# A gated sum moved from a stage of its own into the last group of a state-space mixer

## The reference, cut to what matters

```
attn = mixer(x)                     # in-projection, conv, chunked scan, gate, norm, out-projection
f    = ffn(x)                       # Walsh-Hadamard transforms and two small matmuls
h    = x + attn * silu(f)           # "the joining"
out  = layer1(layernorm(h))         # attention and experts, with a gated sum of its own
```

## Time and profile before

| what | value |
|---|---|
| median of 3 runs | 2561.49 us (2558.56 to 2563.39) |
| the profiled execution | 2560.0 us, of which the trace spans 2557.9 us |
| PE busy | 2264.5 us, 89% of the span |
| DVE busy | 1857.7 us, 73% |
| ACT busy | 1427.6 us, 56% |
| POOL busy | 1275.0 us, 50% |
| granted TensorE clock, mean | 0.950 of full speed |

### The profile page before, as it was taken

The page is one execution under the profiler, slowest core; times in us unless marked ns, Lnnn a source line. Parts: engine busy times, 40 slices in busy tenths (PEclk is TensorE's granted clock), DMA queues, the critical chain, the costliest instruction groups (busy, mean ns, idle before and its releaser), DMA issues. The chain is left out here.

```text
span 2557.9 us, 45525 instructions
## 1 busy us (share of the span) xinstructions
PE 2264.5 (89%) x16164; PEld 1796.8 (70%) x16164; DVE 1857.7 (73%) x3274; ACT 1427.6 (56%) x2439; POOL 1275.0 (50%) x1250
## 2 busy tenths in 40 slices
PE   4994899999999999999999972599999996699993
PEld 2784788888888888888888852488888885344432
DVE  5875777777777777777777746677777776777755
ACT  1331787877878787878787741122222224266661
POOL 3453576787767777686876650345545450000000
PEclk9997999999999999999999985799999998799996
DMA  2002112112121121211211111100000002222214
GB/s 89 1 22 109 42 47 81 44 53 81 53 73 53 44 89 47 78 52 44 82 52 53 44 63 38 30 27 28 21 28 28 21 14 78 74 74 76 80 61 136
DMA packets 91519, 141.18 MB, mean 55 GB/s; under 512 B 23328, under 2 KB 60544, under 8 KB 90048
## 3 DMA queue, kind: packets, MB, share of 16 engines
q1 hardware_dynamic: 89280, 133.96, 15.6%
q10 hardware_dynamic: 2048, 4.72, 0.6%
HBM read 118.12 MB, written 20.32 MB: 54 GB/s over the span
## 5 line engine op out<-in xcount | busy, mean ns | idle before, releaser
L1053 DVE SCALAR_TENSOR_TENSOR mix_cv<-mix_pp,mix_cw,mix_cv 128x384 f32<-128x384 f32 (+4 forms) x864 | 490.9, 571 | 219.3 <-ACT mix_cv L981 198.5
L75 PE MATMUL mix_pp<-l0in_XH,mix_w_lo 128*128 128x384 f32 (+2 forms) x576 | 244.3, 424 | 31.1 <-DVE mix_ss L1042 22.9
L1192 POOL TENSOR_TENSOR ffn_hl<-ffn_h,ffn_hh 128x512 fp32r<-128x512 f32 x112 | 144.8, 1293 | 250.1 <-ACT ffn_hh L1250 250.1
L996 ACT ACTIVATE mix_lm<-mix_pd 128x512 f32<-128x512 f32 x256 | 153.3, 599 | 206.0 <-PE mix_pd L895 204.0
L839 POOL TENSOR_TENSOR mix_ce<-mix_ce,mix_cv 128x1024 f32<-128x1024 f32 x112 | 266.8, 2382 | 0.0
L963 PE MATMUL mix_px<-mix_wo,mix_z 128*128 128x256 f32 x1024 | 256.4, 394 | 0.0
L1715 DVE TENSOR_REDUCE att_tops<-att_psc 128x1 f32<-128x512 f32 (+3 forms) x384 | 189.9, 550 | 56.4 <-PE att_psc L1663 32.2
L845 POOL TENSOR_TENSOR mix_zt<-mix_zsq 128x256 f32<-128x256 f32 x128 | 94.2, 736 | 264.0 <-ACT mix_zsq L1004 264.0
L1739 ACT ACTIVATE att_pr<-att_pst 128x1024 f32<-128x1024 f32 (+7 forms) x256 | 156.5, 656 | 104.0 <-PE att_pst L1680 73.6
L1250 ACT ACTIVATE ffn_hh<-ffn_h 128x512 fp32r<-128x512 f32 x112 | 71.1, 635 | 249.0 <-DVE ffn_h L1273 249.0
L981 ACT ACTIVATE mix_cv<-mix_pp,mix_cb,mix_cw 128x384 f32<-128x384 f32 (+1 forms) x288 | 179.0, 622 | 44.8 <-PE mix_pp L77 44.8
(11 more groups left out here) (330 smaller groups left out, 6893.0 us busy)
## 6 DMA issues: line engine op xcount, KB each, us to landing
mix_ce<-ecs SPq DMA_DIRECT2D x112, 512.0 KB, 3.6
mix_w_raw<-in_w_in SPq DMA_DIRECT2D x8, 1280.0 KB, 5.5
a_part<-att_sums SPq DMA_DIRECT2D x32, 256.0 KB, 5.1
ffn_raw<-in_wgu SPq DMA_DIRECT2D x56, 128.0 KB, 2.2
mix_ll<-cs SPq DMA_DIRECT2D x384, 4.0 KB
mix_wo<-in_w_out SPq DMA_DIRECT2D x8, 512.0 KB, 6.4
ffn_draw<-in_wd SPq DMA_DIRECT2D x28, 128.0 KB, 2.1
q<-qkv_part SPq DMA_DIRECT2D x24, 128.0 KB, 1.9
```

The costliest lines, as they stand in the source:

```text
L75: pe.matmul(out, l_lo, r_hi, start=start, stop=False)
L996: act.activation(lm[o][:, 4 * i:4 * i + 4, :].rearrange("p h l -> p (h l)"), pd[:, :], ACT.Exp).then_inc(l_done, 1)
L1053: last = dve.scalar_tensor_tensor(out, of, cw[:, g, ct, 3 - d:4 - d], out, ALU.mult, ALU.add)
```

## The change

The mixer gets the two arrays f (`f_dram`) and x (`x_dram`) in memory, and in its last group (`LAST` = 112) it forms h row by row. For each token tile i = 0 to 15:

- SP loads row i of f and of x into one of two small buffers each (`load_row`). It does so at the head of iteration c = 113 + i, ahead of that iteration's `rl`, `ll` and `ce`; from i = 2 on it first waits for `joined` >= i - 1, which says that row i - 2 no longer needs the buffer. Row 15 is loaded behind the loop.
- ACT applies Silu to f in slot 113 + i, behind the gate's Silu.
- POOL, at the end of slot 114 + i, waits for the row to be final and multiplies it by silu(f), then adds x and raises `joined`.

`combine` and its tensors are gone.

```diff
+        x0, f0 = ([s.sb(f"{n}{j}", [P, D]) for j in range(2)] for n in ("x0", "f0"))
+        LAST = NC - 16
             # sync
+                def load_row(i):
+                    wait(sp, joined, i - 1)
+                    sp.dma_start(f0[i % 2][:, :], f_dram[:, i, :]).then_inc(f_in[i % 2], 16)
+                    sp.dma_start(x0[i % 2][:, :], x_dram[:, i, :]).then_inc(x_in[i % 2], 16)
...
                         load_weights(g + 1)
+                    if c > LAST:
+                        load_row(c - 1 - LAST)
                     at = slice(b * (T // 2) + j * Q, b * (T // 2) + (j + 1) * Q)
                     wait(sp, d_done, 2 * (c - 1))
                     sp.dma_start(rl[c % 2][0:3, :, :], ...
...
+                load_row(15)
             # gpsimd, at the end of a slot
+                    if LAST <= c - 2 < NC:
+                        i = c - 2 - LAST
+                        pool.wait_ge(acc_done, c - 1)
+                        pool.wait_ge(swished, i + 1)
+                        pool.tensor_tensor(ACC[:, i, :], ACC[:, i, :], f0[i % 2][:, :], ALU.mult).then_inc(product, 1)
+                        pool.wait_ge(product, i + 1)
+                        pool.wait_ge(x_in[i % 2], 16 * (i // 2 + 1))
+                        pool.tensor_tensor(ACC[:, i, :], ACC[:, i, :], x0[i % 2][:, :], ALU.add).then_inc(joined, 1)
             # scalar, behind the gate's Silu
+                    if LAST <= p < NC:
+                        i = p - LAST
+                        act.wait_ge(f_in[i % 2], 16 * (i // 2 + 1))
+                        act.activation(f0[i % 2][:, :], f0[i % 2][:, :], ACT.Silu).then_inc(swished, 1)
...
-def combine(nc, tag, SUM, X, S, F, x_dram, f_dram):
...
-                    act.activation(th[:, r, :], F[:, r, :], ACT.Tanh, scale=0.5).then_inc(th_done, 1)
...
-                    dve.scalar_tensor_tensor(SUM[:, r, :], th[:, r, :], 0.5, X[:, r, :], ALU.mult, ALU.add).then_inc(summed, 1)
```

More of the change, by code:

```diff
@@ L662, in mixer @@
 def mixer(nc, w_in, conv_w, conv_b, d_skip, norm_w, w_out, XH, XL, cs3, ecs_d, sel_rows, one_rows,
-          ident, TDT, TDTD, DCH, ACC):
+          ident, TDT, TDTD, DCH, ACC, x_dram, f_dram):
     NC = G0 * 2 * CPS
@@ L688, in mixer @@
         ll = [s.sb(f"ll{j}", [KD_ROWS, 2, Q], BF16) for j in range(2)]
+        x0, f0 = ([s.sb(f"{n}{j}", [P, D]) for j in range(2)] for n in ("x0", "f0"))
+        x_in, f_in = ([s.sem(f"{n}{j}") for j in range(2)] for n in ("x_in", "f_in"))
+        swished, product, joined = (s.sem(n) for n in ("swished", "product", "joined"))
         pp = [s.bank(f"pp{j}") for j in range(2)]
@@ L1906, in build @@
                 mixer(nc, w_in, conv_w, conv_b, d_skip, norm_w, w_out, XH, XL, cs3, ecs_d, c_sel_rows, c_one_rows,
[L1907 to L1911, removed]
+                      ident, *tabs, X, x_v, f0_d)
         Scope.free_semaphores(nc)
```

## The result

| | before | after |
|---|---|---|
| median, us | 2561.62 (2558.56 to 2563.39, 4 runs) | 2632.39 (2631.33 to 2634.28, 4 runs) |
| span of the profiled execution, us | 2557.9 | 2632.5 |
| granted TensorE clock, mean | 0.950 | 0.941 |

The changed kernel is slower: 1.0283 of the time before, 95% interval 1.0269 to 1.0297. That is 70.8 us between the medians, where 82.5 had been forecast (2644 from the 2561.49 known then, with a range of 2612 to 2668).

A forecast was written before the change was run, and what follows sets the result against it. PE was taken to set the pace in the last group's slots. End -18.3, SP's wait +77.8, ACT +2 and clock +21.5 gave +83 us on 2560.0, so 2643, or 2644 as median; range 2612 to 2668.

The forecast's parts named there:

- The deciding term: Slots 115 to 127: SP's wait for POOL's slot c - 1 holds back PE's tables, 77.8 us in all.
- the landing: Last `ll` of each slot arriving after its issue: 2.0 us, the median of a 48 KB load behind others.
- SP's issue: After POOL's end, SP wakes and issues f, x, `rl` and `ll`, up to the last `ll`'s start: 1.85 us.
- the weight load: On PE ahead of each slot's first matmul, after the tables land: 0.25 us on the chain.
- the 2 us put on ACT: Added Silu, 0.32 us on the chain in six slots where POOL's `rs` waits for ACT's `ss`.
- Nothing in the slot makes up for it: From PE's start to POOL's end all hangs on PE's start, so the delays of 13 slots add.
- The clock: After about 6 us idle, PE's Y starts at 1.2 GHz in each of 13 slots: 13 x 1.65 = 21.5 us.
- the rival of a steady clock: The wait binds in the 13 slots but PE's clock holds: 2622 us; chance 25%.
- The end: After the last row, the 19.88 us joining stage goes and two POOL operations add 1.56 us: -18.3 us.
- The router's table load: ACT needs a table load before the router's exponential; 2.63 us of idle covers it, otherwise under 1.5 us.
- The hidden wait: POOL's joining is done before SP needs the queue, so only the end counts: 2542 us; chance 5%.
- The late landing: Tables behind 256 KB of f and x land in 3.8 us, 1.8 more per slot: 2667 us; chance 10%.

The follow-up runs named there:

- e4: The kernel before, joining stage kept, with only SP's wait for POOL's slot c - 1 ahead of the tables in iterations 115 to 127: 2614.56 us, 1.0224.
- e3: The changed kernel with three buffers of each row instead of two, so SP waits for a joining one slot older: 2536.85 us, 0.9912 of before.
- e5: The changed kernel with twenty matmuls, their result overwritten, ahead of the first decays in slots 115 to 127: 2609.85 us, 1.0194 of before.
- e1: The changed kernel with the row loads and their wait moved to the end of SP's iteration: 2540.11 us, 0.9927 of before.
- e2: The changed kernel with four buffers of each row instead of two, loads in the same place: 2540.11 us, 0.9924 of before.
- e6: The changed kernel with SP's wait kept at the iteration's head, but tables `rl` and `ll` sent ahead of the rows: 2620.33 us, 1.0236 of before.

## Why the prediction was right, point by point

- **The deciding term, a wait on SP in 13 slots: shown.** SP's waits name POOL 13 times, PE's name `ll` 13 times; with the wait alone (e4) the kernel is 2.2% slower, with the event one slot older (e3) it is not slower at all. The Trainium skill (DMA: Bandwidth & Descriptors, "Anatomy of one DMA — SWDGE (gpsimd) path") says, on the path of loads that GpSimd issues, that DMA engines do not wait on semaphores and that the issuing sequencer does, before dispatch. SP's trace agrees: the load of f starts 0.03 us after POOL's end, and `rl` and `ll`, which wait for nothing new themselves, go out only behind it, `rl` 0.89 us after POOL's end.
- **Its size: the landing was the mis-sized term.** From POOL's end to PE's start 5.6 us had been forecast; measured are 63.5 / 13 = 4.89. The two POOL operations (1.5 forecast, 1.48) and SP's issue (1.85 forecast; 1548.54 - 1546.69 = 1.85 to the start of the last `ll`, at 1547.90 + 2/3 of 0.96) are right. The landing with the weight load had been put at 2.0 + 0.25, from the 48 KB load; measured are 1550.01 - 1548.54 = 1.47 in slot 124, and 1.37 to 1.61 over the 13. So 0.78 too much, in 13 slots 10 us: most of the 11.7 us by which the forecast was high; the 2 us put on ACT, below, are most of the rest. No row of the prediction shows the 0.25 of the weight load: before the change that load began 0.21 us ahead of the matmul, after a wait for the tables it begins 0.01 us ahead (1550.00 and 1550.01). Even the lower bound, the 1.8 of the 48 KB load, was too high for 4 KB.
- **Nothing in the slot makes up for it: right.** All 13 delays add; the slots are 17.0 us long on average, inside the 15 to 18 forecast.
- **The clock: right, and its size too.** 21.5 us forecast; the excess of the pieces between first and second decays over before adds up to 22.9 us in the trace, and e5 gives back 22.5. The prediction's doubt was about 6 us without matmuls; after waits of 4.3 to 5.7 us Y ran at a granted clock of 0.50 to 0.58 in every one of the 13 slots. That every step begins cold, which the prediction cites from the Trainium skill (TensorE: Matmul & The Clock Gate, "HAM oscillation — how this bites in real kernels"), agrees with this trace. In e4, after waits of 1.4 to 3.1 us, the clock held through Y in 4 of the 13 slots: there the rival of a steady clock would have been right in part.
- **The end: right.** -18.3 forecast; 1.6 - 19.88 = -18.3 in the trace of the changed kernel, and -18.7 to -22.5 for the whole of e1 to e3, each uncertain by some 5 us.
- **ACT: too dear.** 2 us were put on the Silu ahead of `ss`. From 1384 us to the mixer's end POOL's wait for `ss` is 7.6 us in 10 places, against 7.3 in 9 before, and in e2 the slots start when they did before. The term is 0.3 us or less. The router's table load came, and where it was expected: ACT's idle time before that exponential is now split into the load and a rest.

```profile
1658.75 1.28 ACT L1375 ACT_TABLE_LOAD   x1
1661.37 0.42 ACT L1375 ACTIVATE route_cw<-route_cw 128x256 f32<-128x256 f32 x1 [1.34 <-DVE route_cw L1398]
```

- **The rivals.** The hidden wait was the right answer to another kernel: 2542 forecast for it, and 2537 to 2540 measured once the event is a slot older. The late landing did not come: with the rows ahead, PE starts 1.49 us after the issue of the last `ll` on average, without them 1.39 (e6), so they cost 0.1 us and not 1.8. The condition of the hidden wait, tables that go out some 5 us earlier, is what one more buffer brings (in e3 the last `ll` leaves 5.0 us before its use, of which the landing takes about 1.5).

## What to carry to other kernels

On SP's queue here, a load that had to wait for a buffer held up every load behind it: before putting one into a queue that prefetches, ask how old the event will be when the queue gets there, and put the waiting load last or give it one more buffer (here the difference between 2.8% slower and 0.9% faster). A long wait of the issuing queue says nothing by itself: 95 us of it cost nothing, 191 us cost about 90; look at the time from the issue of what stands behind it to its use. And when TensorE idles several microseconds at the head of each step, price the slower start of the step beside the idle time (here 1.8 us a step beside 5.3).

## What the runs showed that I had not expected

- A 4 KB load on SP's queue wakes TensorE 1.36 to 1.61 us after its issue begins (e4, e6 and the changed kernel); 256 KB sent just ahead of it made that 0.1 us longer on average.
- After waits of 2.1 to 3.1 us the granted clock fell in some slots and not in others, within one run (e4); after 3.2 to 5.7 us Y ran at 0.50 to 0.58 in every slot (e6 and the changed kernel).
- Matmuls whose results are thrown away made the changed kernel 22.5 us faster: Y ran at the clock's upper level again.
